# Opening the value sums with the long products, a 16-column value product, and new orders on every engine

## The reference

```python
q = (x @ Wq).reshape(B, S, HEADS, DIM_HEAD)        # heads: 8 x 64, then 16 x 8
k, v = context @ Wk, context @ Wv                  # context: 154 rows of 96
attn = softmax(q @ k.T * scale);  out = (attn @ v) @ Wo + bo
...
weights, idx = gate(x)                             # top 4 of 16 in groups, then top 2 of 8
g, u = silu(x @ w1.T), x @ w3.T
out = sum over experts of weight * (g * u) @ w2.T, plus shared experts
```

## Time and profile before

| what | value |
|---|---|
| runs | 231.91 us median, 231.86 to 232.44 |
| profiled execution | 234.22 us, its span 232.4 us |
| TensorE's granted clock over the span | 0.993 of full |
| ACT busy | 67% |
| POOL busy | 54% |
| three up-projection products, 324 in all | 128.4 us busy |

### The profile page before, as it was taken

How to read it: one execution, slowest core, us unless ns; L and a number is a source line. 1 busy time by engine, 2 the same in 40 slices (tenths; PEclk the granted TensorE clock), 3 DMA queues, 4 the chain that set the end, 5 groups by cost and what they waited for, 6 DMA issues and landing times.

```text
span 232.4 us, 4647 instructions
## 1 busy us (share of the span) xinstructions
PE 225.3 (97%) x1389; PEld 166.9 (72%) x1389; DVE 164.3 (71%) x482; ACT 155.6 (67%) x378; POOL 125.4 (54%) x126
## 2 busy tenths in 40 slices
PE   7899999999999999999999999999999999999994
PEld 3476765964889898889534563488878887888873
DVE  3589984788667953699846993555867776776874
ACT  2579999987678436662569778876464686744661
POOL 0765742898047927766590305407499500996540
PEclk9999999999999999999889999999999999999999
DMA  6780000000039915800600000018000002700002
GB/s 208 208 288 4 1 3 0 0 3 1 3 87 245 390 63 162 200 3 4 217 3 0 7 0 3 3 37 328 3 0 0 1 3 75 290 0 1 4 0 90
DMA packets 10174, 17.07 MB, mean 73 GB/s; under 512 B 3715, under 2 KB 5540, under 8 KB 9766
## 3 DMA queue, kind: packets, MB, share of 16 engines
q1 hardware_dynamic: 9926, 16.45, 22.9%
q10 hardware_dynamic: 224, 0.32, 0.4%
HBM read 16.08 MB, written 0.62 MB: 72 GB/s over the span
## 4 chain that ended last, share of the span: by engine, by line
PE 80%; ACT 6%; DMA 5%; DVE 3%; SPq 3%; issue 1%; POOL 1%; DVEq 0%; POOLq 0%
PE psum L1169 10%; PE psum L1172 10%; PE psum L1170 10%; ACT prob L747 5%; PE psum L1320 5%; PE psum L1378 5%; PE psum L1327 4%; PE psum L1328 3%; PE psum L1329 3%; PE psum L1429 3%; PE psum L1250 3%; PE psum L1272 3%; PE psum L1282 3%; PE psum L1398 2%; DMA ctxT<-in_ctxT 2%; DMA spread<-cw 2%
## 5 line engine op out<-in xcount | busy, mean ns | idle before, releaser
L701 POOL TENSOR_TENSOR act_s<-act_s,spread 128x512 f32<-128x512 f32 x35 | 44.2, 1290 | 20.2 <-DMA spread<-cw 14.4
L1169 PE MATMUL psum<-xT_hi,w_hi 128*128 128x512 f32 x108 | 43.9, 406 | 0.0
L1172 PE MATMUL psum<-xT_lo,w_hi 128*128 128x512 f32 x108 | 42.3, 391 | 0.0
L1170 PE MATMUL psum<-xT_hi,w_lo 128*128 128x512 f32 x108 | 42.2, 391 | 0.0
L796 ACT CAST q<-psum 128x512 fp32r<-128x512 f32 x35 | 20.4, 586 | 20.4 <-PE psum L1329 13.8
L1005 DVE TENSOR_TENSOR q<-psum,q 128x512 fp32r<-128x512 f32 x35 | 23.8, 687 | 13.4 <-ACT q L796 13.1
L786 ACT ACTIVATE act_s<-psum 128x512 f32<-128x512 f32 x39 | 23.0, 597 | 12.7 <-PE psum L1172 8.3
L1142 DVE TENSOR_REDUCE neg_max<-psum 128x2 f32<-128x308 f32 x64 | 26.3, 472 | 5.8 <-PE psum L1378 5.5
L645 POOL TENSOR_TENSOR w_lo<-w_src,w_hi 128x768 fp32r<-128x768 f32 x12 | 21.7, 1825 | 10.5 <-ACT w_hi L716 10.5
L651 POOL TENSOR_TENSOR rstd<-vareps,minus_half 128x4 f32<-128x4 f32 x8 | 8.1, 1014 | 35.2 <-DVE vareps L906 35.2
L701 POOL TENSOR_TENSOR hid<-hid,spread 128x512 f32<-128x512 f32 x13 | 16.5, 1290 | 18.9 <-DMA spread<-cw 14.6
(11 more groups left out here) (171 smaller groups left out, 470.8 us busy)
## 6 DMA issues: line engine op xcount, KB each, us to landing
spread<-cw SPq DMA_DIRECT2D x16, 256.0 KB, 4.8
spread<-cw SPq DMA_DIRECT2D x6, 512.0 KB, 5.7
w_src<-in_w SPq DMA_DIRECT2D x2, 1152.0 KB, 5.2
w_src<-in_w SPq DMA_DIRECT2D x1, 2304.0 KB, 11.9
spread<-cw SPq DMA_DIRECT2D x8, 128.0 KB, 3.0
w<-in_w SPq DMA_DIRECT2D x1, 576.0 KB, 6.7
out<-X SPq DMA_DIRECT2D x4, 128.0 KB, 1.8
wv<-in_wv SPq DMA_DIRECT2D x2, 192.0 KB, 5.0
```

Of the source, the lines that this page charges most:

```text
L701: pool.tensor_tensor(g, g, spread[:, slot, :], ALU.mult).then_inc(weighed, 1)
L1169: pe.matmul(dst, w_hi, xT_hi[:, b, :], start=True, stop=False)
L1170: pe.matmul(dst, w_lo, xT_hi[:, b, :], start=False, stop=False)
L1172: return pe.matmul(dst, w_hi, xT_lo[:, b, :], start=False, stop=True)
```

## The change

Three things change in the code, and the lists with them.

- `pv1` of groups 0 and 1 now opens the banks (start=True) and waits for them to be free. `rest1` only adds. The banks are taken at `pv1` in the list.
- `vf1` reads only the first 16 of each head's 32 columns of wv1, and writes 256 columns. VectorE copies them in two pieces to where they belong, and POOL clears v1 once at the start (L636 of the new file), since the other halves are never written.
- All lists but SP's are new.

```diff
@@ PROGRAM (a line of each list) @@
-        "kT.0 kT.1 kT.0 kT.2 xT.3 vf.1 vf1.4 q.2 q.3 q.4 xT.2 q.3 scores.4.0 scores.3.1 scores.2.5 scores.6.7 " +
+        "kT.0 kT.1 kT.0 xT.2 kT.1 k1.0 k1.3 q.2 q.4 xT.5 q.2 q.4 scores.1.3 scores.4.2 scores.5.0 scores.6.7 " +
...
@@ bank_uses @@
         elif kind == "rest1":
-            keys = [("pv1", step[1], k) for k in range(2)] if step[2] == 0 else []
+            keys = []
...
         elif kind == "pv1":
-            keys = []
+            keys = [step] if step[2] < 2 else []
@@ gpsimd @@
+            pool.memset(v1[:, :, :].rearrange("p b c -> p (b c)"), 0.0).then_inc(cleared0, 1)
@@ vector, vf1 @@
-                    half = G1 * P // 2
-                    dve.tensor_copy(v1[:, b, 0:half], bank(step)[:, 0:half])
-                    dst, src = (x.rearrange("p (h u c) -> p h u c", u=2, c=PAD // 2) for x in (v1[:, b, half:], bank(step)[:, half:]))
-                    dve.tensor_copy(dst[:, :, 0, :], src[:, :, 1, :])
-                    moved(dve.tensor_copy(dst[:, :, 1, :], src[:, :, 0, :]), step)
+                    dve.wait_ge(cleared0, 3)
+                    dst = v1[:, b, :].rearrange("p (h u c) -> p h u c", u=2, c=PAD // 2)
+                    src = bank(step)[:, 0:H1 * PAD // 2].rearrange("p (h c) -> p h c", c=PAD // 2)
+                    dve.tensor_copy(dst[:, 0:H1 // 2, 0, :], src[:, 0:H1 // 2, :])
+                    moved(dve.tensor_copy(dst[:, H1 // 2:, 1, :], src[:, H1 // 2:, :]), step)
@@ tensor, vf1 @@
-                        ins = pe.matmul(bank(step), ctxT[0:k, step[1], 0:P], w[:, :], start=True, stop=True)
+                        if kind == "vf1":
+                            w = w[:, :].rearrange("k (h c) -> k h c", c=PAD)[:, :, 0:PAD // 2]
+                            dst = bank(step)[:, 0:H1 * PAD // 2].rearrange("p (h c) -> p h c", c=PAD // 2)
+                        else:
+                            w, dst = w[:, :], bank(step)
+                        ins = pe.matmul(dst, ctxT[0:k, step[1], 0:P], w, start=True, stop=True)
@@ tensor, rest1 and pv1 @@
-                        if h == 0:
-                            wait_bank_free(pe, ("pv1", b, g % 2))
...
-                                            start=(h == 0), stop=False, skip_group_check=True, tile_position=(PAD * r, PAD * j))
+                                            start=False, stop=False, skip_group_check=True, tile_position=(PAD * r, PAD * j))
...
+                    if g < 2:
+                        wait_bank_free(pe, step)
...
-                                        start=False, stop=(g >= 2), skip_group_check=True, tile_position=(0, PAD * j))
+                                        start=(g < 2), stop=(g >= 2), skip_group_check=True, tile_position=(0, PAD * j))
```

More of the change, by code:

```diff
@@ L152 @@
     "PE":
[24 rows of a table removed]
-    "ACT":
-        "kT split lnB kT xT kT kT lnB q xT q split " + 16 * "score " +
-        "pT score score pT k1 pT score pT score score split score pv pv score pv pv place_k1 score score " +
-        "score score score split score score place_k1 pT score score place_k1 lnB pT k1 pT xT split k1 pT " +
[3 rows of a table removed]
[L184 to L190, removed]
@@ L191 @@
-    "DVE":
[L192 to L205, removed]
[25 rows of a table added]
@@ new lines @@
+    "ACT":
+        "split kT lnB kT kT xT k1 k1 lnB q xT kT q place_k1 " + 16 * "score " +
+        "pT score score score pT score score pT pT score score score pv pv score split pv pv " + 7 * "score " +
+        "place_k1 place_k1 place_k1 place_k1 pT pT split place_k1 pT k1 lnB pT xT k1 split split gate split " +
+        "pv pv pv pv place_k1 place_k1 place_k1 place_k1 place_k1 h1 h1 place_k1 cwT h1 lnB xT h1 h1 place_k1 " +
+        "gate " + 6 * "h1 " +
+        "place_k1 place_k1 split place_k1 cwT split split split h1 h1 split lnB xT h1 qd h1 q1copy q1copy " +
+        "q1copy q1copy h1 h1 split mT h1 " + 8 * "exp " +
+        "lnB expR xT expR qd split mT q1copy q1copy q1copy q1copy expR exp expR exp exp exp split split od " +
+        "exp exp exp exp mT od exp exp onT exp exp exp mT exp exp exp expR expR expR lnB expR xT " + 8 * "exp " +
+        "route od od h1 cwT h1 hsplit h1 h1 onT h1 h1 h1 hsplit h1 " + 3 * "h1 hsplit " +
+        "lnB h1 xT h1 h1 hsplit hsplit h1 hsplit hsplit h1 route hsplit hsplit h1 cwT h1 hsplit hsplit h1 h1 " +
+        "hsplit hsplit h1 h1 h1 h1 h1 hsplit h1 hsplit hsplit hsplit h1 ycopy hsplit h1 h1 ycopy h1 hsplit " +
+        "hsplit hsplit hsplit h1 h1 hsplit hsplit " + 3 * "hsplit hsplit h1 " + "hsplit h1 hsplit hsplit ycopy ycopy ",
@@ new lines @@
+    "DVE":
+        "lnA sel lnA xT q k1 k1 q xT " + 9 * "score " +
+        "norm score q q q score norm score score vf pT score pT norm q score score vf1 pT score norm score " +
+        "score pT score vs score pT pT pT score pT norm score score score norm " + 7 * "score " +
+        "pT norm pT wo pT pT norm wo lnA pT pT vf pT k1 pT xT vs1 gate route route route route wo wo lnA k1 " +
+        "h3 xT gate h3 " + 3 * "h3 route " + "h3 h3 h3 route h3 vf1 res lnA h3 xT h3 qd h3 h3 score1 score1 h3 " +
+        15 * "score1 " + "h3 h3 h3 score1 h3 score1 res lnA " + 9 * "score1 " + "xT score1 score1 score1 score1 qd " +
+        20 * "score1 " + "oT " + 6 * "score1 " + "oT " + 6 * "score1 " +
+        "wo1 wo1 lnA xT gate route route oT h3 oT h3 hsplit wo1 wo1 h3 lnA " + 4 * "hsplit h3 " +
+        "xT h3 hsplit hsplit gate h3 route hsplit h3 hsplit route h3 hsplit hsplit h3 h3 h3 h3 hsplit hsplit " +
+        "hsplit hsplit h3 h3 h3 h3 hsplit h3 h3 hsplit hsplit hsplit h3 hsplit h3 h3 hsplit hsplit h3 h3 " +
+        "hsplit hsplit h3 hsplit h3 hsplit hsplit h3 h3 h3 hsplit hsplit h3 hsplit h3 hsplit hsplit h3 hsplit " +
+        "h3 hsplit hsplit res h3 res res res last_res last_res ",
@@ L206 @@
     "Pool":
-        "lnA split lnA bo bo split " + 7 * "norm " + "lnA norm place_k1s split split split lnA place_k1s " +
-        8 * "weigh " + "split split lnA " + 8 * "weigh " +
-        "split split lnA split place_k1s place_k1s split split split lnA split split weigh weigh weigh weigh " +
-        "weigh lnA " + 27 * "weigh ",
+        "lnA split lnA place_k1s " + 6 * "norm " +
+        "bo norm norm lnA split split place_k1s split bo split place_k1s lnA weigh weigh weigh split weigh " +
@@ L211 @@
+        "place_k1s weigh weigh weigh weigh split split lnA weigh weigh weigh weigh split weigh weigh weigh " +
+        "split weigh split lnA split split split split lnA weigh weigh weigh weigh weigh lnA " + 27 * "weigh ",
     "SP":
```

## The result

The new kernel takes 233.06 us (median of 20 runs, 232.31 to 233.93), the kernel before 231.99 (20 runs, 231.56 to 233.42): a ratio of 1.0038, 95% interval 1.0025 to 1.005. The forecast was 231.0 and faster. The sign was wrong, and the value lies just outside the range.

A forecast was written before the change was run, and what follows sets the result against it. The prediction took TensorE, busy 97% of the span, as the bound, plus few stretches where it stands or runs slow. Terms 0.00 + 0 - 1.1 + 0.15 = -0.95, rounded to -0.9, gave 231.0 us, range 229.6 to 233.0.

The forecast's parts named there:

- I carry the difference over to that median unchanged: The sum was made against the profiled execution of 234.22 us, and its difference applied to the runs' median of 231.91.
- the term of -1.1: From the last routed product to batch 1's first score: that score at 121.7 instead of 122.81, so 1.1 us gained.
- the stage before 98: Between 20 and 98 us the forecast counted nothing for stands of TensorE.
- The forecast's own sign for this stage: The forecast would be wrong if TensorE stood over 1 us anywhere between 20 and 98.
- The third rival: ACT held in front of cwT by a cast waiting for 2.3 MB, or queued silus delaying h1's banks: 233.0 us, chance 0.16.
- Values' product: Value product of 256 instead of 512 columns: 0.43 us less for each batch, 0.86 for both.
- The start: Kernel's opening: work behind 10.32 unchanged (0.00); first queries 0.2 us later, taken as 0, range 0 to +0.3.
- The copy, the maxima, the transposes, the first score: Batch 1's cwT copy at 85.6, maxima from 97.95, their transpose at 105.4, xn's transposes at 115.8, first score at 121.7.
- The stands before the transposes: In front of the transposes of xn (L1225), TensorE was to have no stand over 0.4 us.
- the first rival: The slow clock stays, since stands of 0.2 to 0.7 us remain: +1.3, 232.3 us, no change, chance 0.17.
- The tail: After the last down-projection: both last down-products stand behind y's last transposes, so the final additions come 0.15 us later.
- Second rival: VectorE's second-half maxima and the chain through oT, onT and wo1 set that stage's end: 231.9 us, chance 0.14.

The follow-up runs named there:

- b_again: The kernel before, unchanged, profiled a second time: 232.09 us with a span of 230.3 and the granted clock at 1.00.
- b_pool: The kernel before with POOL's second split of w_1 moved ahead of the layer norm of batch 0: 232.97 us, ratio 1.0037.
- b_narrow: The kernel before with its old lists and only the narrower value product (256 columns instead of 512): 231.69 us, ratio 0.9971.
- b_less_cover: The kernel before with two TensorE products, h3.1.1.4 and h1.1.1.6, moved from ahead of qd.0 to behind it: 233.22 us, ratio 1.0042.
- a_all: The new kernel, TensorE's order kept, with ACT's cwT copy and silus ahead of w_1 casts and POOL's second w_1 split behind batch 1's weighings: 231.65 us.
- a_rest_opens: The new kernel with rest1 opening the banks again, ahead of the pv1 products, in both batches: 238.31 us.

## Why the prediction was wrong, point by point

- **The step that failed first: "I carry the difference over to that median unchanged".** The profiled execution stood at 234.22 us, and no run shown was above 232.44. Its half clock, priced by the forecast as regained, is absent in five of six executions of the kernel before. From 121 to 103 left it cost 1.3 us over an ordinary execution, 3.86 against 2.55. Another 0.8 us of that profile's excess is spread over the stages before 121 left. An ordinary execution had its first score of batch 1 at 120.72 (b_again); the new kernel's came at 121.83, so the term of -1.1 was +1.1 against it. Against its own execution the sum came out (234.22 less 0.95 is 233.3, measured 233.09), in part by luck: from 139 to 121 left the new kernel lost 1.3 us more than that profile, which the sum didn't have, and before 139 left 0.7 less, which it didn't have either.
- **The step that failed second: the stage before 98, where I counted "nothing" for TensorE.** It costs 1.6 us. The late cwT was forecast and came (84.24 for the cast, 85.43 for the copy; 21.9 us behind batch 0's, forecast 21.6). The forecast's own sign for this stage, a stand of over 1 us, did not show either: the longest was 0.83. The third rival had the place right ("ACT held in front of cwT", "the silus queued behind delay h1's banks") at 0.16, but its 233.0 is near the 233.06 by luck: its 2 us were to come on top of 231.0, and the 2304 KB transfer landed on time (84.24, forecast 84.3). It did not have POOL's split ahead of the statistics, which alone is worth 0.9 us in b_pool. I had taken POOL's list as covered because POOL is 54% busy.
- Values' product: 0.43 us less each, right. But a saving of TensorE in front of a wait for POOL is no saving: b_narrow kept half.
- The start: first queries at 10.85, against 10.88 in the first profile and 10.56 in the second. In the range of 0 to 0.3.
- The copy, the maxima, the transposes, the first score: 85.43, 97.66, 105.17, 115.76, 121.83, forecast 85.6, 97.95, 105.4, 115.8, 121.7. Idle behind q1: 0.68, forecast 0.6. These were right as times, though they were compared with a disturbed profile, whose own steps came 0.3 to 2.1 us later than in an ordinary execution.
- The stands before the transposes: forecast under 0.4 us, measured 0.45 for ACT, and bank waits beside it. The clock at 1.00 throughout, right; the first rival (the slow clock stays) is refuted for this kernel by 32 executions.
- The tail: forecast +0.15. From 7 us of work left on, the new kernel loses 0.1 more than b_again. Right, and below what can be told.
- Second rival (VectorE's maxima keep the time): refuted by b_less_cover and a_all, where what is lost or gained before the maxima arrives at the end in full.

## What to carry to other kernels

Compare the profiled execution with the run list before building on it: if it lies above all runs, find its excess (here a stretch at half clock, and 0.8 us elsewhere) and leave it out of what a change can gain. When orders change, count on every engine what now stands ahead of each producer on the chain, POOL too: here one split of 1.8 us running beside a statistic cost 0.9 us at the end. When removing one stand moves it along the same chain, list all that lengthened the chain and take it away at once: one at a time, the repairs gave 0.4 us at most, which is within the noise, together 1.0. Test the parts of a change one by one: the narrow product alone did as well as the whole change with its repairs.

## What the runs showed of the hardware

- A four-column tensor_scalar on VectorE took 1.59 and 1.12 us beside a split on POOL, 0.17 without one. The aggregation just ahead of it took 0.38 us beside the split (86.83, new kernel) and in b_again without one.
- The half clock isn't a property of a kernel but has a chance in each execution: 21 of 127 of the kernel before had it, none of 32 of the new one, all 6 of a_rest_opens. Before it could fall, TensorE was busy from 112 on for 1.51 and 1.49 of 2.00 us in two profiles of the kernel before, of which only the first fell; for 1.55 in the new kernel and 0.63 in a_rest_opens. In the kernel before, an execution that had it was 1.2 us longer.
- A product of 97 rows that reads 16 of every 32 columns took 0.43 us for 256 columns, half of the 0.86 for 512.
